# A macaron transformer layer on one core: zero rows by GpSimd memsets, splits of row maxima on VectorE, and another order of loads and steps

## The reference

```python
x = x + 0.5 * ffn(layernorm(x), W1, b1, W2, b2)
x = x + attn(layernorm(x), Wq, bq, Wk, bk, Wv, bv, Wo, bo)
x = x + 0.5 * ffn(layernorm(x), W1, b1, W2, b2)
# ffn:  W1 (512x128), W2 (128x512) quantised to -1, 0, 1 by their mean absolute value
#       relu(x @ W1q.T + b1) @ W2q.T + b2
# attn: 16 heads of 8; q and k rotated (rope); softmax(q k / sqrt(8)) v; @ Wo.T + bo
```

## Time and profile before

| | us |
|---|---|
| three runs | 539.21, 543.53, 546.67 |
| median | 543.53 |
| the profiled execution | 541.95 |
| its span, first to last instruction | 540.2 |
| busy: TensorE, VectorE, ScalarE, GpSimd | 498.2, 393.5, 334.9, 217.6 |
| GpSimd power over 128x4 (L1017), mean of one | 1.04 |
| GpSimd addition over 128x512 (L1027), the one at 14.48 | 1.27 |

### The profile page before, as it was taken

How to read it: one execution, slowest core, us unless ns; L and a number is a source line. 1 busy time by engine, 2 the same in 40 slices (tenths; PEclk the granted TensorE clock), 3 DMA queues, 4 the chain that set the end, 5 groups by cost and what they waited for, 6 DMA issues and landing times.

```text
span 540.2 us, 8600 instructions
## 1 busy us (share of the span) xinstructions
PE 498.2 (92%) x3187; PEld 235.9 (44%) x3187; DVE 393.5 (73%) x579; ACT 334.9 (62%) x425; POOL 217.6 (40%) x292
## 2 busy tenths in 40 slices
PE   6686899989999989998999979999999999999986
PEld 3454434343453535352454533354435433443445
DVE  5672886957887678875787758877977898698124
ACT  2411346748857676765857655868686768577751
POOL 3403358434565183805552183418431831103202
PEclk7996889999999999998999998999999999999999
DMA  7859317402460139003360039013801480000000
GB/s 217 213 195 204 69 32 224 100 2 77 151 129 2 33 107 233 5 2 112 125 137 1 23 118 232 5 31 112 224 12 40 150 186 3 21 2 3 1 21 21
DMA packets 20681, 48.27 MB, mean 89 GB/s; under 512 B 2528, under 2 KB 5088, under 8 KB 19616
## 3 DMA queue, kind: packets, MB, share of 16 engines
q1 hardware_dynamic: 19328, 45.89, 32.0%
q10 hardware_dynamic: 1312, 1.84, 1.1%
HBM read 20.58 MB, written 18.87 MB: 73 GB/s over the span
## 4 chain that ended last, share of the span: by engine, by line
PE 62%; POOL 9%; DMA 8%; issue 7%; DVE 7%; ACT 5%; SPq 1%; POOLq 0%; ACTq 0%; DVEq 0%
PE heads_acc L575 17%; PE unit L558 11%; PE unit L539 11%; PE side L637 7%; DMA q_stack<-q_scratch 3%; DVE maxima L863 3%; PE side L631 3%; ACT probs L778 3%; PE side L617 2%; PE side L625 2%; PE side L613 2%; POOL normed_ffn L376 2%; DMA q_scratch<-q_parts 2%; DMA k_swap<-k 1%; PE heads_acc L645 1%
## 5 line engine op out<-in xcount | busy, mean ns | idle before, releaser
L863 DVE TENSOR_REDUCE maxima<-unit 128x2 f32<-128x1024 f32 x256 | 305.5, 1220 | 97.1 <-PE unit L539 96.1
L778 ACT ACTIVATE probs<-unit 128x1024 f32<-128x1024 f32 x256 | 256.6, 1027 | 112.1 <-PE unit L558 111.3
L575 PE MATMUL heads_acc<-probs,v_heads 128*32 128x512 f32 x1024 | 136.6, 611 | 1.3 <-ACT probs L778 1.1
L558 PE MATMUL unit<-q_stack,k_stack 64*128 64x512 f32 x512 | 119.9, 467 | 9.9 <-DMA q_stack<-max_T 5.7
L539 PE MATMUL unit<-k_stack,q_stack 62*128 62x512 f32 x512 | 115.3, 448 | 8.6 <-DMA q_stack<-q_scratch 5.7
L558 PEld LDWEIGHTS unit<-q_stack,k_stack 64*128 64x128 f32 x512 | 48.7, 187 | 79.4 <-issue 31.7
L539 PEld LDWEIGHTS unit<-k_stack,q_stack 62*128 62x128 f32 x512 | 49.7, 190 | 56.8 <-ACT probs L778 26.4
L1033 POOL TENSOR_SCALAR max_parts<-maxima 128x16 fp32r<-128x16 f32 x31 | 6.3, 205 | 129.5 <-DVE maxima L863 129.2
L637 PE MATMUL side<-w_q,hidden 128*128 128x128 f32 x416 | 57.2, 289 | 0.0
L637 PEld LDWEIGHTS side<-w_q,hidden 128*128 128x128 f32 x416 | 50.6, 197 | 13.6 <-issue 11.3
L575 PEld LDWEIGHTS heads_acc<-probs,v_heads 128*32 128x32 f32 x1024 | 21.0, 108 | 44.3 <-issue 36.1
(11 more groups left out here) (143 smaller groups left out, 443.5 us busy)
## 6 DMA issues: line engine op xcount, KB each, us to landing
k_scratch<-k_parts SPq DMA_DIRECT2D x16, 512.0 KB, 3.0
q_scratch<-q_parts SPq DMA_DIRECT2D x14, 512.0 KB, 2.8
k_stack<-k_scratch SPq DMA_DIRECT2D x14, 512.0 KB, 7.0
q_stack<-q_scratch SPq DMA_DIRECT2D x14, 512.0 KB, 9.4
resid<-in_x SPq DMA_DIRECT2D x8, 256.0 KB, 5.1
k_stack<-zero_rows SPq DMA_DIRECT2D x4, 480.0 KB
q_stack<-zero_rows SPq DMA_DIRECT2D x4, 480.0 KB
k_swap<-k SPq DMA_DIRECT2D x14, 128.0 KB, 2.3
```

The costliest lines, as they stand in the source:

```text
L558: mm = pe.matmul(to[:, e, :], k_stack[part, quad // NQ % 2, pair, kt * P:(kt + 1) * P], q_stack[part, quad // NQ % 2, pair, :], start=True ...
L575: mm = pe.matmul(heads_acc[32 * j:32 * j + 32, :], v_heads[:, b % 2, at, ODD * odd:ODD * odd + 32], probs[:, burst % RING, j, :], start=(k ...
L778: act.activation(probs[:, burst % RING, 2 * pp:2 * pp + 2, :], unit_of(PLACE["exp", n]), ACT.Exp, scale=SCALE).then_inc(s_exp, 1)
L863: dve.tensor_reduce(maxima[:, quad % 2, :, r], unit_of(PLACE["max", k]), AX_X, ALU.max).then_inc(s_max, 1)
```

## The change

- The zero rows are no longer written by eight DMAs. GpSimd sets each slot of each stack (128x4096 words) to zero by a memset before the rows are loaded: k's slot 0 first of all, k's slot 1 and both of q's later. The memset of `v_heads` moves behind the first reciprocal deviation.
- VectorE does the splits of the maxima, right behind the last maximum of the quad.
- SyncE issues all of x before the rows of -1. It waits until the first quad's rows have landed before it issues the other rows of batch 0.
- `max_row` of the next batch's first quad goes ahead of `swap("k", b + 2)`.
- More fills: 10 for 4 before the first scores, 14 for 8 before the first "e", and three groups of 4 in the first steps.
- The three tables place the steps anew.

```diff
-FILL_BEFORE_MAX = 4
+FILL_BEFORE_MAX = 10
-FILL_BEFORE_EXP = 8
+FILL_BEFORE_EXP = 14
+FILL_BESIDE_EXP = 4
 STEADY = [
-    "e m ffn1_T", "e m pv heads_copy1@-1 ffn1_up0", "e m", "e heads_T1@-1 pv m", "e m ffn1_up1 pv max_T1 ffn1_stats@5",
...
+    "e m ffn1_T", "e m", "e pv m heads_copy1@-1 ffn1_up0", "e m pv max_T1", "e m", "e heads_T1@-1 pv m", "e m pv",
...
             load_x(2)
-            sp.wait_ge(s_row_values, 2)
+            for j in range(3, B):
+                load_x(j)
+            sp.wait_ge(s_row_values, 1)
+            sp.wait_ge(s_zeros["k"], 2)
             for e in range(2):
...
                 sp.dma_start(to, minus_rows[:].unsqueeze(1).to_broadcast([PARTS, 2 * NPAIR, S])).then_inc(s_rows_fill, 16)
-            zero_between(0)
-            for j in range(3, B):
-                load_x(j)
...
                 rows_to_stack(sp, "k", 0, e, slice(0, 2), s_stack_first)
+            sp.wait_ge(s_stack_first, STACK_LANDED)
+            sp.wait_ge(s_zeros["q"], 2)
             stack(0, slice(2, NPAIR), s_stack[0])
-            zero_between(1)
...
-                if on("proj", b):
-                    swap("k", b + 2)
                 if on("values", b):
                     max_row((b + 1) * NQ)
                 if on("proj", b):
+                    swap("k", b + 2)
                     swap("q", b + 2)
...
+                    elif use[0] == "fill":
+                        pe.wait_ge(s_first_maxT, use[1])
+                        fill(FILL_BESIDE_EXP)
...
                     act.wait_ge(s_scratch["q"], 16 * PARTS)
+                    act.wait_ge(s_zeros["q"], 1)
...
                 dve.tensor_reduce(maxima[:, quad % 2, :, r], unit_of(PLACE["max", k]), AX_X, ALU.max).then_inc(s_max, 1)
+                if quad == 0 and r % T == T - 1:
+                    split_first_max(r // T)
+                elif quad > 0 and r == QSTEPS - 1:
+                    split_max(quad)
...
+            def zeros(n, slot):
+
+                tile = q_stack if n == "q" else k_stack
+                pool.memset(tile[:, slot, :, :].bitcast(F32), 0.0).then_inc(s_zeros[n], 1)
+
+            zeros("k", 0)
+            pool.wait_ge(s_minus_half, 1)
+            ln_rstd("ffn1", 0)
             pool.memset(v_heads[:], 0.0).then_inc(s_v_fill, 1)
...
             add_bias("ffn1", 0)
+            zeros("k", 1)
...
             add_bias("ffn1", 1)
+            zeros("q", 0)
+            zeros("q", 1)
```

More of the change, by code:

```diff
@@ L44 @@
 STACK_LANDED = 16 * 4
-ROWS_FILLED = (16 * (2 + 4), 16 * (2 + 8))
+ROWS_FILLED = 16 * 2
 ROPE_STEPS = 5
@@ L236, in macaron_layer @@
         s_rows_fill = sem("stack_rows_filled")
+        s_zeros = {n: sem(f"{n}_stack_slots_set_to_zero") for n in "qk"}
         s_v_fill = sem("v_heads_filled_with_constants")
@@ L417, in load_x @@
                 sp.dma_start(batch_rows(j), x[j].rearrange("(p t) d -> p t d", t=T)).then_inc(s_x[j], 16)
[L419 to L424, removed]
             load_x(0)
@@ L531, in scores_of @@
                     pe.wait_ge(*stacked(*divmod(quad, NQ)))
-                    if quad == NQ:
-                        pe.wait_ge(s_rows_fill, ROWS_FILLED[1])
                 if (free := unit_free(PLACE["max", k])) is not None:
@@ L664, in _ @@
             fill(FILL_BEFORE_MAX)
-            pe.wait_ge(s_rows_fill, ROWS_FILLED[0])
+            pe.wait_ge(s_rows_fill, ROWS_FILLED)
             for k in range(OPEN_MAX):
@@ L818, in _ @@
                         take_heads(use[2] * 2 + use[1])
+                    elif use[0] == "fill":
+                        continue
                     else:
@@ L852, in ln_stats, with split_first_max, split_max @@
                     dve.bn_aggr(mean_var[n][:, t, :], stats[n][:, t, :]).then_inc(s_var[n], 1)
+            def split_first_max(p):
+                dve.wait_ge(s_max, (p + 1) * T)
+                whole = maxima[:, 0, :, p * T:(p + 1) * T]
+                dve.tensor_scalar(first_parts[:, p, :, 0, :], whole, 1.0, 0.0, ALU.mult, ALU.add).then_inc(s_first_split, 1)
+                dve.wait_ge(s_first_split, p * SPLIT_STEPS + 1)
+                dve.tensor_tensor(first_parts[:, p, :, 1, :], whole, first_parts[:, p, :, 0, :].bitcast(F32),
+                                  ALU.subtract).then_inc(s_first_split, 1)
+            def split_max(quad):
+                dve.wait_ge(s_max, (quad + 1) * QSTEPS)
+                wait(dve, s_maxT_psum, quad - 1)
+                whole = maxima[:, quad % 2, :, :]
+                dve.tensor_scalar(max_parts[:, :, 0, :], whole, 1.0, 0.0, ALU.mult, ALU.add).then_inc(s_split, 1)
+                dve.wait_ge(s_split, (quad - 1) * SPLIT_STEPS + 1)
+                dve.tensor_tensor(max_parts[:, :, 1, :], whole, max_parts[:, :, 0, :].bitcast(F32),
+                                  ALU.subtract).then_inc(s_split, 1)
             def max_of(k):
@@ L898, in _ @@
             dve.memset(minus_rows[:], -1.0).then_inc(s_row_values, 1)
-            dve.memset(zero_rows[:], 0.0).then_inc(s_row_values, 1)
             dve.memset(minus_half[:], -0.5).then_inc(s_minus_half, 1)
@@ L1027, in add_bias @@
                 pool.tensor_tensor(xb[n][:], batch_rows(j), bias.to_broadcast([P, T, D]), ALU.add).then_inc(s_xb[n], 1)
-            def split_max(quad):
-                pool.wait_ge(s_max, (quad + 1) * QSTEPS)
-                wait(pool, s_maxT_psum, quad - 1)
-                whole = maxima[:, quad % 2, :, :]
-                pool.tensor_scalar(max_parts[:, :, 0, :], whole, 1.0, 0.0, ALU.mult, ALU.add).then_inc(s_split, 1)
-                pool.wait_ge(s_split, (quad - 1) * SPLIT_STEPS + 1)
-                pool.tensor_tensor(max_parts[:, :, 1, :], whole, max_parts[:, :, 0, :].bitcast(F32),
-                                   ALU.subtract).then_inc(s_split, 1)
-            def split_first_max(p):
-                pool.wait_ge(s_max, (p + 1) * T)
-                whole = maxima[:, 0, :, p * T:(p + 1) * T]
-                pool.tensor_scalar(first_parts[:, p, :, 0, :], whole, 1.0, 0.0, ALU.mult, ALU.add).then_inc(s_first_split, 1)
-                pool.wait_ge(s_first_split, p * SPLIT_STEPS + 1)
-                pool.tensor_tensor(first_parts[:, p, :, 1, :], whole, first_parts[:, p, :, 0, :].bitcast(F32),
-                                   ALU.subtract).then_inc(s_first_split, 1)
+            def zeros(n, slot):
[4 more added lines that the diff above has]
+            ln_rstd("ffn1", 0)
             pool.memset(v_heads[:], 0.0).then_inc(s_v_fill, 1)
@@ L1085, in _ @@
                     ln_rstd("ffn2", b - 1)
-                if b > 0:
-                    split_max(b * NQ + 2)
                 if b == 0:
@@ L1095, in _ @@
                     ln_apply(pool, "attn", b + 2)
-                if b < B:
-                    split_max(b * NQ + 3)
                 if b == 0:
```

13 lines of the change are left out of this document (removed), and 32 rows, old and new, of tables (FIRST, LATER, STEADY).

## The result

The changed kernel takes 560.3 us (median of four, 558.5 to 562.2) against 541.9 (four runs, 539.2 to 546.7): 1.033 times as long, interval 1.024 to 1.042. Forecast were 531 us and a range up to 543, with 0.07 for slower. The profiled execution has a span of 559.5 us, 19.3 more than before, at a mean clock of 0.957 (before 0.965).

A forecast was written before the change was run, and what follows sets the result against it. The prediction saw TensorE nearly full in the steady part, losing time to late first scores, waits and half clock. Its terms summed to -11.1 us, 541.95 - 11.1 = 530.9, so 531 us; range 520 to 543.

The forecast's parts named there:

- The tables: Steps placed anew in every batch: same work in another order, most transposes of maxima up to two steps earlier; 0 us.
- this sign: Closing sign of failure: the new tables bring waits of their own; no price given.
- The swaps: Batch ends: maxima issued ahead of k's swap remove three waits of 1.6 us (-4.8) and half clock behind one (-1.6).
- The splits: Splits on VectorE: +3.0 for its added small instructions, -1.1 for a wait near 320 us, -2.0 for half clock behind it.
- rival 5: Quad ends: splits held beside GpSimd keep VectorE from freeing score banks, TensorE stops; over 2% slower, e.g. 557 us; chance 0.07.
- The memsets: Start: the first memset, of v_heads, blocks VectorE's first normalisation at 7.8 us and delays all that follows; +2.7 us.
- Rival 2: Start: memsets of q's tile also block VectorE's normalisation near 24 us, two times 3.55, giving 538 us; chance 0.20.
- The argument against: Against rival 2, at the start: VectorE's pieces follow each other without a gap and may keep what they hold.
- First rows alone: Start: q's first rows land sooner without the bulk beside them, first scores at 43.5 instead of 46.88 us; -3.4 us.
- warm start: Start: first score pairs nearer 1.52 us apart (-1.9); more fills keep 62 to 73 us at full clock (-2.0).

The follow-up runs named there:

- e1: The changed kernel with the tables STEADY and LATER of the kernel before; 549.2 us, 1.016.
- e12: The kernel of e11 with the splits of the maxima on VectorE as changed; 535.2 us, 0.990.
- e2: The changed kernel with three waits on GpSimd, so that memsets start only after VectorE's scaling before them is done; 549.2 us, 1.014.
- e13: The changed kernel loading only pairs 0 to 3 of each next batch's stack (1 MB instead of 2), leaving out part of the computation; 540.0 us, 0.999.
- e17: The kernel of e2 with the next stack loaded in two halves, the second behind the rows of max_T2; 529.8 us, 0.982.
- e6: The kernel before with only the rows of max_T4 issued ahead of the swap of k; 549.9 us, 1.015.
- e9: The kernel before with the changed start alone (memsets, FIRST, first quad's rows alone) and the three GpSimd waits of e2; 541.2 us, 1.000.
- e11: The kernel of e9 with the rows of max_T4 ahead of k's swap in batches 0 to 3 alone; 537.9 us, 0.995.
- e5: The kernel before with only the splits of the maxima moved to VectorE, behind the last maximum of their quad; 550.0 us, 1.015.
- e10: The kernel of e9 without the three GpSimd waits, so the start alone as it was changed; 552.6 us, 1.020.
- e4: The kernel before, its start kept, with the changed STEADY and LATER, splits on VectorE and max_T4's rows ahead of the swaps; 560.1 us, 1.032.
- e18: The kernel of e12 with the next stack loaded in two halves, the second behind the rows of max_T2; 528.4 us, 0.980.
- e7: The changed kernel with ScalarE issuing the rows of max_T2 on its own queue in batches 1 to 7; 562.7 us, 1.038.

## Why the prediction was wrong

**The tables, costed at 0.** This is the step that failed first: "Steps placed anew. I cost it at 0". The new tables cost 11 us from e1 to the changed kernel (1.016 to 1.033) and 14 from e12 to e2, where each goes with its own order of swaps. The prediction closed with this sign, waits that the new tables bring, and gave it no price. What it had wrong is the transfer that the moved step meets. `max_T2` came up to two steps earlier. Its rows were issued 7.4 to 10.2 us behind the start of the stack's load in batches 1 to 6 before, and 2.9 to 7.2 in the changed kernel; in batches 5 and 6 the load itself also starts some 4 us later in the batch. As the rows are usable only when the load has landed, and step 16 comes sooner too, `max_T2` waits for the rest of the load in batches 2 to 6. I had counted the waits that the change removes, and not asked where in SyncE's order, and beside which transfer, each moved step issues its DMAs. e13 and e17 show the mechanism from both sides. One wait of this kind was in the trace before already, the fourth and smallest of the earlier trace rows, at step 16 of batch 5, 0.4 us behind the landing of the last load (issued at 383.20, 10.9 us):

```profile
394.46 0.49 PE L558 MATMUL unit<-q_stack,k_stack 64*128 64x512 f32 x2 [0.80 <-DMA q_stack<-max_T]
```

**The swaps, costed at -4.8 and -1.6.** The waits at batch ends go, as it said, but -6.4 was too much: in batches 1 to 3 it is -2.6 in e6, where step 16 takes some back, and -4.3 from e9 to e11. The rows it was read from were the ends of batches 1 to 3; the old LATER has its steps the other way round, and there the order costs 9.7. Alone the part is +8. In the changed kernel LATER fits the order, so this loss is not in its 560 us.

**The splits, costed at +3.0 - 1.1 - 2.0.** Alone +8 (e5), and -2.7 with the new FIRST and swaps by table (e12 against e11). The mechanism of rival 5 is real: both instructions of 0.17 us held to 1.2 us, and TensorE 1.66 us for a score bank behind them, in two places of the changed kernel. But it strikes 6 of 62, not every quad, and in e1 and e5 it holds `attn_out` as well, which no term had. That the holding is what makes e5 slower fits its waits, but no run took it away alone. The page named in the prediction (the Trainium skill, SBUF — State Buffer, "Who interferes with whom") has the second of the two contend where GpSimd reads SBUF; 1.19 us at 382.98 agrees.

**The memsets, costed at +2.7.** The first did what was taken (3.23 instead of 1.11). Rival 2 came too, from q's tile (8.76 instead of 2.06), and so did k's second half (5.38 instead of 2.12), which no case had. The argument against, that VectorE's pieces keep what they hold, is refuted by the row at 26.25. Together 11 us (e2, and e9 against e10), where 2.7 and for rival 2 9.8 were said. The same section says that whoever issues first has the port pair for the whole instruction. The trace agrees in that no piece beside a memset ends before it does. It adds something: drawn one by one, the first piece begins at 26.25 beside the addition and ends only behind both memsets, 8.19 us later, so as drawn a piece that waits is not let in between two GpSimd instructions either.

**First rows alone and warm start, -3.4, -1.9 and -2.0.** The first two came: 3.4 us from loads to scores instead of 7.6, pairs 1.52 apart, and 11.7 us from the first scores to the first exponential instead of 14.1. Of the third the clock came (1.00), but its 2.0 us are not shown: batch 0 lasts 68.1 us instead of 70.3, and in e9, with the same start and the splits on GpSimd, 71.6. With the memsets held the first exponential is 4.0 to 4.9 us earlier. But e9 ends where the kernel before ends: a lead at the start is worth only what the waits behind it leave.

In one order of adding, the start as changed is 1.020 (e10), splits and swaps on it bring 1.016 (e1), the tables 1.033. In the other, splits, swaps and tables alone give 1.032 (e4) and the start adds nothing. With the start held, splits and swaps by table bring 0.990 (e12) and the new tables 1.014 (e2). The parts aren't additive, and no split of the 18 us into fixed shares would be true. A profiled start also differs by some us with the clock: e6, whose start is that of before, ran 45 to 60 us at 0.54 instead of 0.77, and its first exponential came 2.5 us later. e4 has the old start too, 0.51 in the same stretch and a first exponential 3.2 us later than before, so some 3 us of its loss may be that.

Two things are luck. The forecast gave 0.07 to slower, all of it to rival 5, which is only a small part of the loss. And e17 and e18 end near the forecast of 531 us, by an edit to the load that the prediction did not have.

## What to carry to other kernels

Where a table of steps moves, go through each moved step's DMAs and ask what is in their queue or in flight at the new time: 16 KB that a matmul waits for must not follow 2 MB that nobody needs yet. Another queue for the small one did not help here (e7). If such a load can be neither ahead nor behind, cut it and let the small one through the middle. A memset on GpSimd belongs behind VectorE's critical pieces, by a wait if need be. And a saving read at one batch's end holds only for batches whose table has the same order.

## What the runs showed of the hardware

- A GpSimd memset of 128x4096 (3.5 us) held VectorE's scaling of 128x128 from 0.34 us up to 3.59, an addition of 1.27 us and one memset 4.80, and an addition and two memsets 8.19. These are the two pieces of the changed kernel that began beside each (ns min/median/max; the median is the mean of the two):

```profile
L376 DVE TENSOR_SCALAR normed_ffn<-resid,mean_var_ffn,rstd_ffn x2: 3592/4198/4803, 16.0 to 17.3; 128x128 f32<-128x128 f32 x2
L376 DVE TENSOR_SCALAR normed_attn<-resid,mean_var_attn,rstd_attn x2: 7042/7614/8185, 26.3 to 27.5; 128x128 f32<-128x128 f32 x2
```

  (The two of a pair overlap in the drawing, so where one ends and the next begins may be told wrongly.)
- 16 KB issued 3.4 us behind the first of four loads of 512 KB were usable after 9.4 us, and after 7.8 from another engine's queue, in both cases when the last of the four had landed. The four took 12.6 us from first issue to last landing. Swaps of 128 KB take 2.3 us in the median.
- ScalarE's two issues for the rows took it 3.44 us in batch 1 of e7 and 1.28 in batch 5.
